# The first stage's output bias as two one-row products in PSUM, its rows copied by ScalarE, and its first score maxima in pairs on half rows

## The reference, cut to what matters

```python
h = jnp.einsum('bsd,ed->bse', x, W_in) + b_in
# scan over the tokens:  s = s * decay + B_p * xt ;  y = C_p * s
out = jnp.einsum('bse,fe->bsf', y, W_out) + b_out
mu = out.mean(-1, keepdims=True)
var = out.var(-1, keepdims=True)
return (out - mu) * jax.lax.rsqrt(var + LN_EPS) * gamma + beta
...
x = _layernorm(x + first_stage)
scores = jnp.einsum('bhnd,bhmd->bhnm', q, k) * scale
attn = jax.nn.softmax(scores, axis=-1)
```

## Time and profile before

| | |
|---|---|
| median of 3 runs | 887.32 us (886.73 to 890.37) |
| the profiled execution | 887.83 us |
| its span in the trace | 886.0 us |
| TensorE busy | 858.0 us (97%) |
| VectorE busy | 568.2 us (64%) |
| ScalarE busy | 363.5 us (41%) |
| GpSimd busy | 563.5 us (64%) |
| mean granted TensorE clock | 0.993 |

### The profile page before, as it was taken

One profiled execution on the slowest core, in us unless ns is written; L12 is line 12 of the kernel. 1 busy time (PEld: TensorE's weight loads), 2 busy tenths in 40 slices (PEclk: granted clock), 3 DMA queues, 4 the chain that ended last, 5 costly groups with the idle time before them and its releaser, 6 DMA issues.

```text
span 886.0 us, 12719 instructions
## 1 busy us (share of the span) xinstructions
PE 858.0 (97%) x4798; PEld 506.8 (57%) x4798; DVE 568.2 (64%) x1149; ACT 363.5 (41%) x510; POOL 563.5 (64%) x366
## 2 busy tenths in 40 slices
PE   9998899999999999999999999999998999999994
PEld 4654545555556555555455455555577888885441
DVE  4798757667757677666677675675676736335553
ACT  3254434434435444434445443345364224323332
POOL 0354298898896898896888896988301053323444
PEclk9999999999999999999999999999999999999998
DMA  9213300000001000000100000104099011483420
GB/s 268 71 47 103 113 1 1 24 1 1 1 1 48 24 1 2 1 1 25 44 4 1 1 1 1 48 1 166 7 232 374 13 48 48 143 279 120 130 74 19
DMA packets 44141, 55.12 MB, mean 62 GB/s; under 512 B 3625, under 2 KB 35121, under 8 KB 44081
## 3 DMA queue, kind: packets, MB, share of 16 engines
q1 hardware_dynamic: 37840, 46.16, 16.5%
q0 software_dynamic: 2688, 6.31, 2.0%
q10 hardware_dynamic: 3552, 1.84, 0.7%
HBM read 36.44 MB, written 18.89 MB: 62 GB/s over the span
## 4 chain that ended last, share of the span: by engine, by line
PE 88%; DVE 9%; ACT 1%; issue 1%; POOL 0%; POOLq 0%; ACTq 0%
PE st L806 23%; PE av L828 21%; PE mx L792 8%; PE bt L1447 4%; PE bg L1437 3%; PE bu L1437 3%; PE bgu L1708 3%; PE misc L773 3%; PE misc L845 2%; PE bank_a L392 2%; PE bank_a L415 1%; PE bgu L1705 1%; PE by L1708 1%; PE br L1447 1%; PE misc L859 1%; PE mx L859 1%
## 5 line engine op out<-in xcount | busy, mean ns | idle before, releaser
L611 POOL TENSOR_TENSOR accG<-accG,probs 128x1024 f32<-128x1024 f32 (+1 forms) x170 | 405.4, 2385 | 38.6 <-ACT probs L633 23.5
L633 ACT ACTIVATE probs<-st 128x1024 f32<-128x1024 f32 (+1 forms) x208 | 212.8, 1026 | 203.2 <-PE st L806 196.8
L678 DVE TENSOR_REDUCE mxp<-mx 128x1 f32<-128x512 f32 x360 | 232.0, 686 | 60.1 <-PE mx L792 54.6
L828 PE MATMUL av<-probs,V 128*64 128x512 f32 (+1 forms) x832 | 191.7, 598 | 0.0
L792 PE MATMUL mx<-K_hi,Q_hi 64*128 64x512 f32 (+1 forms) x480 | 137.8, 380 | 0.0
L828 PEld LDWEIGHTS av<-probs,V 128*64 128x64 f32 (+1 forms) x832 | 55.5, 136 | 105.7 <-issue 83.9
L806 PE MATMUL st<-Q_hi,K_hi 64*128 64x512 f32 (+1 forms) x416 | 112.7, 444 | 0.9 <-ACT probs L633 0.9
L792 PEld LDWEIGHTS mx<-K_hi,Q_hi 64*128 64x128 f32 x480 | 73.9, 184 | 51.9 <-issue 26.8
L806 PE MATMUL st<-M,ones_r 64*128 64x512 f32 (+1 forms) x416 | 101.2, 393 | 0.0
L806 PE MATMUL st<-Q_hi,K_lo 64*128 64x512 f32 (+1 forms) x416 | 96.8, 393 | 0.0
L806 PE MATMUL st<-Q_lo,K_hi 64*128 64x512 f32 (+1 forms) x416 | 94.5, 394 | 0.0
(11 more groups left out here) (259 smaller groups left out, 1348.0 us busy)
## 6 DMA issues: line engine op xcount, KB each, us to landing
w_gate_up<-in_gate_up SPq DMA_DIRECT2D x4, 2048.0 KB, 12.4
w_down<-in_down SPq DMA_DIRECT2D x2, 2048.0 KB, 9.6
scratch_sorted_x<-zero SPq DMA_DIRECT2D x6, 514.0 KB, 7.8
xs<-scratch_sorted_x SPq DMA_DIRECT2D x24, 128.5 KB, 2.5
scratch_base<-zero SPq DMA_DIRECT2D x6, 512.0 KB, 9.8
base<-scratch_base SPq DMA_DIRECT2D x24, 128.0 KB, 2.1
xring<-in_x SPq DMA_DIRECT2D x4, 512.0 KB, 9.0
scratch_x1b<-xT SPq DMA_DIRECT2D x4, 512.0 KB, 2.9
```

What stands on the lines that cost most here:

```text
L611: pool.tensor_tensor(total[0:r], so_far[0:r], probs[0:r, place(S, t)], ALU.add).then_inc(g_add, 1)
L633: act.activation(probs[0:r, place(S, t)], st[g % 2][0:r, :], ACT.Exp, scale=DH ** -0.5).then_inc(a_probs, 1)
L678: dve.tensor_reduce(mxp[:, F % 2, h * QT + i, j:j + 1], mx[h][:, 0:kn], AX.X, ALU.max).then_inc(v_mx, 1)
L828: mm = pe.matmul(av[h * DH:(h + 1) * DH, :], V[0:r, t, (2 * p + h) * DH:(2 * p + h + 1) * DH], probs[0:r, place(S, t), h * QC:(h + 1) * QC ...
```

## The change

The row b_out is split once on VectorE into `bias_high` and `bias_low`, each on one partition (two instructions of 1x256 beside the scaling of W_out). Each of the 16 `out_proj` gets two more products of 256 columns into the same bank: a column block of ones (one row of `ones_r`) by `bias_high`, and by `bias_low`. The addition on VectorE (L336) is gone; ScalarE copies the bank to `z` instead (`out_rows`), first in each slot. VectorE's statistics and TensorE's next use of the bank wait for that copy.

The zeroed `Q_alone` and its two ScalarE copies are gone. Pieces read `Q_hi` and `K_hi` on the 64 partitions of their head and stand in pairs, one of each head, one in bank 3, one in bank 2; each of the two waits for the maximum of its own bank. One pair stands ahead of the unit of keys or values in slots 17 to 29 and a second one at the end of slots 24, 26 and 28. Before, a slot had pieces on both sides of the unit. The 32 pieces end in slot 29 in both.

```diff
-                    do(piece, next(pieces, -1), PIECES)
+                    do(piece, next(pairs, -1), PIECES // 2)
                 if t < len(kv):
                     kind, u = kv[t]
                     do(key if kind == "k" else val, u, 16)
-                if t > 16:
-                    do(piece, next(pieces, -1), PIECES)
                 if t < len(kv) and kv[t][0] == "k":
                     do(low, kv[t][1], 16)
-                if t >= THREE_FROM:
-                    do(piece, next(pieces, -1), PIECES)
+                if t >= TWO_PAIRS_FROM and t % 2 == 0:
+                    do(piece, next(pairs, -1), PIECES // 2)
...
-                for h in range(2):
-                    rows = slice(DH * h, DH * h + DH)
-                    act.activation(Q_alone[rows, h], banks[1][rows, :], ACT.Copy).then_inc(a_q0, 1)
+            def out_rows(t):
+                act.wait_ge(p_out, t + 1)
+                act.activation(z[:, t], banks[2 + t % 2][:, 0:D], ACT.Copy).then_inc(a_z, 1)
...
+                    dve.tensor_copy(bias_high[:], rows[0:1, 0, :]).then_inc(v_bhi, 1)
...
+                if n == SCALE_AT + 1:
+                    dve.wait_ge(v_bhi, 1)
+                    dve.tensor_tensor(bias_low[:], rows[0:1, 0, :], bias_high[:].bitcast(F32), ALU.subtract).then_inc(v_bias, 1)
...
-                dve.wait_ge(p_out, t + 1)
-                dve.tensor_tensor(z[:, t], banks[2 + t % 2][:, 0:D], rows[:, 0, :], ALU.add).then_inc(v_z, 1)
-                dve.wait_ge(v_z, t + 1)
+                dve.wait_ge(a_z, t + 1)
...
-                dve.wait_ge(a_q0, 3)
+                dve.wait_ge(a_q0, 1)
...
                 if t >= 2:
-                    pe.wait_ge(v_z, t - 1)
+                    pe.wait_ge(a_z, t - 1)
+                if t == 0:
+                    pe.wait_ge(v_bias, 1)
...
+                for part in (bias_high, bias_low):
+                    mm = pe.matmul(banks[2 + t % 2][:, 0:D], mem["ones_r"][0:1, :], part[:], start=False,
+                                   stop=(part is bias_low), skip_group_check=True)
...
-                if n >= 2:
-                    pe.wait_ge(v_mx0, n - 1)
-                pe.matmul(banks[2 + (n + 1) % 2][:, 0:kn], Q_alone[:, h, i * P:(i + 1) * P], K_hi[:, 0, k0:k0 + kn],
-                          start=True, stop=True).then_inc(p_mx0, 1)
+                for h in range(2):
+                    rows = slice(DH * h, DH * h + DH)
+                    if m:
+                        pe.wait_ge(v_mx0, 2 * m + h - 1)
+                    pe.matmul(banks[3 - h][:, 0:kn], Q_hi[rows, i * P:(i + 1) * P], K_hi[rows, 0, k0:k0 + kn],
+                              start=True, stop=True).then_inc(p_mx0, 1)
```

More of the change, by code:

```diff
@@ L85, in before_attention @@
         d_x1T = [sem(f"d_x1T{i}") for i in range(2)]
-        prep = sem("prep")
+        prep, v_bhi = sem("prep"), sem("v_bhi")
         a_exp = sem("a_exp")
         p_in, a_u, v_scan = sem("p_in"), sem("a_u"), sem("v_scan")
-        p_out, v_z = sem("p_out"), sem("v_z")
+        p_out, a_z = sem("p_out"), sem("a_z")
+        v_bias = sem("v_bias")
+        bias_high, bias_low = sb("bias_high", [1, D], F32R), sb("bias_low", [1, D], F32R)
         v_link = sem("v_link")
@@ L117, in do @@
                     f(n)
-            pieces = iter(range(PIECES))
+            pairs = iter(range(PIECES // 2))
             for t in range(len(kv) + 4):
@@ L400, in out_proj @@
                 if t >= 2:
-                    pe.wait_ge(v_z, t - 1)
+                    pe.wait_ge(a_z, t - 1)
+                if t == 0:
+                    pe.wait_ge(v_bias, 1)
+                    pe.wait_ge(g_const, 6)
                 for k in range(DK):
-                    mm = pe.matmul(banks[2 + t % 2][:, 0:D], state[:, k, t * P:(t + 1) * P], w_out[:, k, :],
-                                   start=(k == 0), stop=(k == DK - 1))
+                    pe.matmul(banks[2 + t % 2][:, 0:D], state[:, k, t * P:(t + 1) * P], w_out[:, k, :],
+                              start=(k == 0), stop=False, skip_group_check=True)
+                for part in (bias_high, bias_low):
+                    mm = pe.matmul(banks[2 + t % 2][:, 0:D], mem["ones_r"][0:1, :], part[:], start=False,
+                                   stop=(part is bias_low), skip_group_check=True)
                 mm.then_inc(p_out, 1)
@@ L446, in query, with piece @@
                 mm.then_inc(p_q0, 1)
-            def piece(n):
-                u, j = n // len(KC), n % len(KC)
-                h, i = u // QT, u % QT
+            def piece(m):
+                i, j = m // len(KC), m % len(KC)
                 k0, kn = KC[j]
-                if n == 0:
-                    pe.wait_ge(v_z, TILES)
-                    pe.wait_ge(a_q0, 3)
+                if m == 0:
+                    pe.wait_ge(a_z, TILES)
+                    pe.wait_ge(a_q0, 1)
                     pe.wait_ge(a_khi, len(KC))
-                if n >= 2:
-                    pe.wait_ge(v_mx0, n - 1)
-                pe.matmul(banks[2 + (n + 1) % 2][:, 0:kn], Q_alone[:, h, i * P:(i + 1) * P], K_hi[:, 0, k0:k0 + kn],
-                          start=True, stop=True).then_inc(p_mx0, 1)
+                for h in range(2):
+                    rows = slice(DH * h, DH * h + DH)
[3 more added lines that the diff above has]
+                              start=True, stop=True).then_inc(p_mx0, 1)
             slots(out=out_proj, key=key, val=val, tr=transpose, query=query, piece=piece)
@@ L879, in tensor_part @@
             pe.wait_ge(mem["a_t"], TILES)
-            pe.wait_ge(mem["g_const"], 7)
+            pe.wait_ge(mem["g_const"], 6)
             for S in range(STEPS):
```

28 lines of the change are left out of this document (11 added, 17 removed).

## The result

The changed kernel takes 898.46 us (median of 6 runs, 896.88 to 898.93), the kernel before 887.07 in the same comparison. The ratio is 1.0121 with a 95% interval of 1.0104 to 1.0138: about 10.7 us slower, 9.2 to 12.2 by the interval; the two medians are 11.4 us apart. The forecast was 896.9 us, +9.6. The execution that was profiled took 898.93 us, its span is 897.1 us, 11.1 more than the 886.0 of before.

What follows compares the result with a forecast made beforehand. TensorE was taken as the bound, nearly full in the first stage, with VectorE 2.6 us late at slot 16. `Q_lo` 6.7 us later plus 2.9 for the pairs made +9.6, 896.9 us; range 890.5 to 900.5, own case 894.3 to 899.8.

Steps and rivals of the forecast that it cites:

- one of its own signs of being wrong: After the first stage: the forecast is wrong if the stretch behind 104 us changes length by more than 1 us.
- Term 1: Slots 0 to 15: two one-row bias products cost TensorE 0.59 us a tile; queries end 9.3 us later.
- the first rival: Bias products: one row doesn't change the array's form, so 0.24 us a tile and 891.3 us; chance 0.13.
- Preparation: Before the first tile's bias: splitting the bias on VectorE makes TensorE's first wait cost 0.1 us.
- Term 2: Handover at slot 16: VectorE, relieved of 6.7 us, wins back only its 2.6 us lateness; `Q_lo` starts 6.7 us later.
- Term 3 behind slot 21: Slot 21 to stage end: twelve dearer pairs cost 2.0 us and longer waits for maxima 0.9, +2.9 in all.
- the three waits: After slots 24, 26 and 28, TensorE waits 1.0, 1.0 and 1.2 us for maxima between consecutive pairs, 3.2 in all.
- Term 3 in slots 17 to 20: Slots 17 to 20: VectorE is the bound with the same instructions in the same order, so no change.

Runs made afterwards that it cites:

- the run with 128 partitions: Changed kernel with its two bias products padded to 128 partitions, same columns and count; 891.88 us, ratio 1.0058.
- the pairs alone: Changed kernel's half-row pairs in their new places, with the bias added by VectorE as in the kernel before; 891.41 us, ratio 1.0056.
- the early `Q_lo`: Kernel with one padded bias product and the old pieces, edited to copy `Q_alone` from `Q_hi`, so `Q_lo` waits for `Q_hi` alone; 887.29 us, ratio 1.0005.

## Why the prediction was right, and where not

**Direction and size held, and the mechanism in its main terms**: +9.6 was forecast, +10.7 measured (11.4 between the medians), within the range and within the forecast's own 894.3 to 899.8. One term that the forecast put at nothing was 1 us, and one of its own signs of being wrong came up, for a reason that it had left out (the clock).

- *Term 1, the price of a one-row product.* Forecast 0.59 us a tile, measured 0.63 ahead of keys, 0.62 ahead of values and 0.57 to 0.59 ahead of transposes, split as forecast: 0.25 of columns, 0.38 for the two changes of form (0.35 was taken). From `out_proj(0)` to the end of the queries that makes 50.78 - 41.30 = 9.5 us, against 9.2. That one row would cost what 64 and 16 rows cost was assumed, since no row of before showed one; it held. The reading of the earlier trace rows was bolder than it looks: the load behind the pieces names ScalarE's `probs` as what ended its idle time, so the row alone doesn't part that wait from the change of form. Slot 22 bears the 0.58 us out without such a wait: 2.14 - 1.34 - 0.22. The Trainium skill, TensorEngine Tiling (Array Packing), section Key Properties, says that a change of tiling mode drains TensorE; the run with 128 partitions puts 0.38 us on it. The other rule of the Trainium skill that was weighed, TensorE: Matmul & The Clock Gate, section Step-by-step: what each phase is for, that a weight load's time doesn't depend on rows, holds for the load itself (0.18 us with one row, 0.19 with 128), but says nothing of the changes around it; the first rival rested on that alone and fell.
- *Preparation* was mis-sized: 0.1 forecast, 0.24 measured as a wait in front of `out_proj(0)`. The 1x256 instructions take 0.26 and 0.39 us; the cast takes 0.27 with 128 partitions (in the run with 128 rows). Both stand ahead of TensorE's first wait.
- *Term 2, what VectorE's relief is worth.* Forecast: only the lateness at slot 16, 2.6 us. Measured 9.78 - 7.24 = 2.5. The run without bias products shows the same from the other side: free relief of 6.7 us wins 1.2 to 1.7. That the two `Q_alone` copies cost nothing was right while VectorE was late; once it is on time it stands idle for 0.3 to 1.6 us until they are done, as the runs that kept them show.
- *Term 3 behind slot 21*: forecast +2.9, measured 26.92 - 24.31 = +2.6. Its parts: form 1.6 (forecast 2.0), places 1.0 (forecast 0.9). A pair was dearer where nothing waits (+0.21 a slot instead of +0.17) but not in all twelve places, and the three waits were a little shorter (0.94, 0.94 and 0.99 us against 1.0, 1.0 and 1.2).
- *Term 3 in slots 17 to 20*: forecast nothing, measured 14.18 - 13.13 = +1.05 without a fall of the clock, and 14.10 with the pairs alone. This is the step that failed: "VectorE has the same instructions in the same order in slots 17 to 20, and it is the bound there: no change". It has two holes. The stretch doesn't end with VectorE but with TensorE's slot 20, and there the pair's second half waits for its own maximum and the pair changes the form: 2.30 - 1.81 = 0.49 us. The other 0.56 is VectorE's, by the time at which TensorE's wait in slot 20 ends, 84.66 - 72.78 = 11.88 us behind `Q_lo` against 77.30 - 65.98 = 11.32. Its instructions are the same ones, but two of them take longer beside GpSimd's additions (0.55 and 0.93 us against 0.47 and 0.62, 0.39 together), and it stands idle for 0.16 us before `K_lo` at 81.18, whose keys came behind a dearer pair. With the pairs alone the same idle time and the same 0.93 us stand there, and the wait ends 11.80 us behind `Q_lo`: this comes with the pairs and not with the bias. The run with full-row pairs has no such idle time, and there TensorE's wait in slot 20 ends 11.28 us behind `Q_lo`; but its first instructions also escape GpSimd's additions, because its `Q_lo` is late, so it doesn't part the two. The run with GpSimd's additions cut short, which gains 1.2 us, shows what such slowing costs in all; by the durations 0.4 of it is new.
- *The clock* was left out of the forecast. It is why the two profiled executions differ by 12.54 us at the end of the stage and by 11.1 at the end, so the mark that the prediction set itself, no more than 1 us of change behind 104 us, was missed (1.4 us) by a fall of the clock and not by attention, whose 15 steps take 503.0 us before (606.44 - 103.42) and 503.1 after (619.06 - 115.96). How many falls a median carries on each side differs from comparison to comparison, so sizes under 1.5 us are taken from traces here and not from medians.

Predicted 9.6; add 0.5 for Term 1 with its preparation, 1.05 for slots 17 to 20, take 0.3 for the rest of Term 3: 10.9, against 10.7 by the ratio and 11.4 between the medians; closer than that the measurement doesn't tell. What stays open is what decides where a fall of the clock comes; filling one wait didn't settle it. None of the versions that keep the bias beats the kernel before: the best, with one product for it and the early `Q_lo`, is at 1.0005.

## What to carry to other kernels

Before work is moved from one engine to another, find how late the giving engine is at the next handover: that, and not the sum of what is moved, is the gain, here 2.5 us out of 6.7. A small product with few rows between products with 128 costs more than its columns; padding it with zeros to their form made it 0.38 us cheaper a time, and putting both halves of a split constant on two rows of one padded product halved the rest. And where work is regrouped, ask of each part which buffer it waits for: two products that write two banks and stand together wait for the later of the two readers.

## What was new on the hardware

- Two changes of the array's form around a group of products cost 0.38 us with one row, with one product in the group as with two; two half-row products of 400 columns overlap and still cost 0.21 us more in a full-row neighbourhood than two full-row ones.
- Behind waits of TensorE of 0.9 to 2.5 us the granted clock sometimes goes to the lower level and sometimes not, in the same kernel. The wait of 2.36 us that ends at 678.63 us in the kernel before stands in all 13 profiled executions; seven have a fall behind it, six have none. Where TensorE sets the pace such a stretch costs 1.5 us, and in the shadow of VectorE's chain it cost nothing (the pairs alone, slot 17).
- The mean granted clock of a run counts these falls, and the time goes with it in some versions: of the run without bias products, those at 0.995 took 884.7 to 885.0 us, and those at 0.993 or below 885.7 to 886.8. In the kernel before it says little: beside that run, seven runs at 0.991 took 886.7 to 887.6 us, and 17 at 0.993 took 885.4 to 887.9.
- VectorE's instructions with two full tensors in SBUF take up to 1.03 us instead of 0.48 while GpSimd adds (0.55 and 0.62 in two places, 0.83 to 1.03 in the others); with GpSimd's additions cut to one column all of them take 0.50 or less between slot 16 and slot 21.
